# Decoder layer (Mamba, cross-attention, experts) on one core: the first batch's state scans move from the Mamba stage into the attention's opening

## The chip, the cores and the metric

One core of one Trainium2 chip runs the whole layer in one launch. The metric is the device time of a run in microseconds (us), median of the runs shown. Engines are named as the profile names them: PE (TensorE matmul), DVE (VectorE), ACT (ScalarE), POOL (GpSimd), SP (SyncE, which here only issues DMAs).

## The reference, cut to what matters

```
x: (4, 512, 256) f32        ctx: (4, 1601, 256) f32
x = layernorm(x + mamba(x))            # d_inner 512, 16 states, conv 4, dt_rank 16
x = layernorm(x + xattn(ctx, x))       # 16 heads of 64; keys = [LN(ctx); LN(x)], 2113 of them
x = layernorm(x + experts(x))          # 8 experts, top 2, and 2 shared

mamba:  xz = x @ W_in.T ; conv, silu ; dt = softplus(...) ; B, C per state
        for t: h = exp(dt*A) * h + dt*B*xs ;  y = sum over 16 states of h*C
        out = (y + xs*D) * silu(z) @ W_out.T
xattn:  kv = [LN(ctx); LN(x)] @ Wkv ; q = LN(x) @ Wq ; softmax(q k / 8) v @ Wout
```

## The kernel before

Three stages follow one another: `mamba`, `attention`, `experts`. Everything is f32; the products of the attention's projections are made from a high and a low f32r part of each operand.

**Mamba stage.** A loop over the four batches (x[0] to x[3]) computes, with 512 channels as four blocks of 128 partitions and 512 tokens along the free axis, the gate z, B and C, y0 = xs*D, dt and du = dt*xs. For the batches 0 to 2 these are stored to DRAM (`kept_z`, `kept_bc`, `kept_y`, `kept_dtu`). For batch 3 (`LAST`) the recurrence is run on the spot: for each of the 16 states PE spreads the rows of B and C over the partitions (L368, through the constant `sel`), ACT copies B and makes the decays (L243, L247), POOL multiplies du by B (L181, 128x2048), DVE runs one scan over 128x2048 (L326) and multiplies by C out of PSUM (L332), and PE sums into `ps_y` through the identity (L423). Then gate, output product (L433), residual and layernorm (L340 to L358).

**Attention stage.** Batches are taken in the order `BATCHES = [3, 0, 1, 2]`, 16 heads each: 64 groups g (batch, head) of 17 key tiles kt, which the text calls slots. All engines walk one list written at trace time, `MADE = BEFORE + BESIDE[g][kt] + AFTER`; an engine skips the items that do not concern it and takes the others strictly in this order. Items: S/A (statistics of context rows), N (normalise rows, L983), T (turn them on PE into `ring`, scale and split on ACT, L852 and L856, low part on DVE, L1008, which is also where `ring_free` is counted up), Q/K/V (projections, L1144), X (PE scores and DVE row maxima over the keys, L1188 and L1042), M (maxima to a row), O (output projection), P (Mamba's output product), G/J/L (norm after Mamba and the latents' statistics), E/F (norm after attention). In the main loop PE makes per slot the scores (L1246, L1247), the items of the slot, and the product with the values three slots back (L1259).

**The scans of the later batches** are spread over the main loop of the batch before, 64 units of 128x512 (unit u: block u//16, state u%16), one every `U_STEP` = 2.85 slots: D(u) is POOL's product with B (L795) and ACT's decay (L882); H(u), two slots later, is DVE's scan (L992) followed on POOL by the product with C (L802) and the addition to `y` (L806). POOL runs D and H in the order of the list, so D(u+1) stands behind H(u). B and C of a unit come by a DMA that spreads two rows over the partitions (`load_bc`, 512 KB per unit).

**The opening of the attention** (`BEFORE`): statistics, N and T of all rows; POOL splits the weights in 12 steps (L818, L820), three per block of four heads, each block stored to DRAM before the buffer is used again; then Q, all K, X, M and six V of the first head.

Of the kernel before, what the change touches and what calls it, by code (L numbers as in the profile page):

```python
# [15 lines left out]
F32 = mybir.dt.float32  # L16
# [6 lines left out]
P = 128  # L23
# [9 lines left out]
KEPT = {}  # L33


def mamba(nc, x, w_in_t, conv_w, conv_b, w_x_t, w_dt_t, b_dt, a_log, d_skip, w_out_t, x1):
# [7 lines left out]
    LAST = B - 1  # L44
# [5 lines left out]
    with ExitStack() as ctx:  # L50
# [7 lines left out]
        ps_y = ctx.enter_context(nc.psum_tensor("m_y", [P, CT, S], F32))  # L58
# [4 lines left out]
        wout = sb("m_wout", [P, CT, DM])  # L63
# [3 lines left out]
        a_neg = sb("m_a", [P, CT, NS])  # L67
        dsk = sb("m_d", [P, CT])
        ident = sb("m_ident", [P, P])
        diag_d = sb("m_diag", [P, CT, P])  # L70
        sel = sb("m_sel", [P, 2 * NS, P], BF16)
        x_in = sb("m_xin", [P, TT, DM])
        x_res = sb("m_xres", [P, TT, DM])
# [6 lines left out]
        xdr = sb("m_xdr", [P, S])  # L80
        xd3 = sb("m_xd3", [P, 3, S], BF16)
# [4 lines left out]
        dA = sb("m_dA", [P, 2, CT, S])  # L86
        bsb = sb("m_bsb", [P, 2, S])
        dbx = sb("m_dbx", [P, 2, CT, S])
        h = sb("m_h", [P, 2, CT, S])
        y0 = sb("m_y0", [P, CT, S])  # L90
        stats = sb("m_stats", [P, TT, 6])
        mv = sb("m_mv", [P, TT, 2])
        rstd = sb("m_rstd", [P, TT])
        half = sb("m_half", [P, TT])

        w_loaded = sem("m_w_loaded")
        a_loaded = sem("m_a_loaded")
        x_loaded = sem("m_x_loaded")
        xres_loaded = sem("m_xres_loaded")
        x_in_free = sem("m_x_in_free")  # L100
        consts_set = sem("m_consts_set")
        a_set = sem("m_a_set")
# [12 lines left out]
        dA_ready = sem("m_dA_ready")  # L115
        dbx_ready = sem("m_dbx_ready")
        h_scanned = sem("m_h_scanned")
        y_added = sem("m_y_added")
        g_ready = sem("m_g_ready")
        var_ready = sem("m_var_ready")  # L120
        rstd_ready = sem("m_rstd_ready")
# [10 lines left out]
        def _(sp):  # L132
# [5 lines left out]
            sp.dma_start(wout[:], w_out_t.rearrange("(c p) n -> p c n", p=P)).then_inc(w_loaded, 16)  # L138
            sp.dma_start(x_in[:], x[0].rearrange("(t p) d -> p t d", p=P)).then_inc(x_loaded, 16)
            sp.dma_start(x_res[:], x[LAST].rearrange("(t p) d -> p t d", p=P)).then_inc(xres_loaded, 16)  # L140
            for b in range(LAST):
                sp.wait_ge(x_in_free, b + 1)
                sp.dma_start(x_in[:], x[b + 1].rearrange("(t p) d -> p t d", p=P)).then_inc(x_loaded, 16)
# [11 lines left out]
            sp.wait_ge(z_kept, 16 * LAST)  # L155
            sp.wait_ge(bc_kept, 32 * LAST)
            sp.wait_ge(y0_kept, 16 * LAST)
            sp.wait_ge(dt_kept, 16 * LAST)
            sp.wait_ge(du_kept, 16 * LAST)

        @block.gpsimd
        def _(pool):
            nc.gpsimd.memset(wx[:], 0.0)
            nc.gpsimd.memset(wdt[:], 0.0).then_inc(consts_set, 1)
            nc.gpsimd.memset(ident[:], 0.0)
            nc.gpsimd.memset(sel[:], 0.0)
            nc.gpsimd.memset(half[:], -0.5)
            nc.gpsimd.memset(xs_pad[:], 0.0)
            nc.gpsimd.memset(dA[:, :, :, 0:1], 0.0).then_inc(consts_set, 1)
            pool.wait_ge(consts_set, 2)  # L170
            nc.gpsimd.affine_select(out=ident[:], in_=ident[:], compare_op=ALU.not_equal, fill=1.0, base=0,
                                    pattern=[[-1, P]], channel_multiplier=1)

            nc.gpsimd.affine_select(out=sel[:], in_=sel[:], compare_op=ALU.not_equal, fill=1.0, base=-DTR,
                                    pattern=[[-1, 2 * NS], [0, P]], channel_multiplier=1).then_inc(consts_set, 1)

            def times_b(n, i):
                pool.wait_ge(act_read, B * AREAD + n + 1)
                if n >= 2:
                    pool.wait_ge(h_scanned, n - 1)  # L180
                nc.gpsimd.tensor_tensor(dbx[:, i], du[:], bsb[:, i:i + 1, :].to_broadcast([P, CT, S]),  # L181
                                        ALU.mult).then_inc(dbx_ready, 1)

            pool.wait_ge(du_ready, B)
            for n in range(NS):
                times_b(n, n % 2)
            pool.wait_ge(var_ready, 1)
            nc.gpsimd.tensor_tensor(rstd[:], mv[:, :, 1], half[:], ALU.pow).then_inc(rstd_ready, 1)

        @block.scalar  # L190
        def _(act):
            act.dma_start(a_neg[:], a_log).then_inc(a_loaded, 16)
            for dst, src in ((cb, conv_b), (bdt, b_dt), (dsk, d_skip)):
                act.dma_start(dst[:], src).then_inc(w_loaded, 16)
            act.wait_ge(a_loaded, 16)
            nc.scalar.activation(a_neg[:], a_neg[:], ACT.Exp).then_inc(a_set, 1)
            act.wait_ge(w_loaded, 16 * 8)
            act.wait_ge(consts_set, 3)
            act.wait_ge(a_set, 2)
            for b in range(B):  # L200
# [19 lines left out]
                if b < LAST:  # L220
                    if b > 0:
                        act.wait_ge(y0_kept, 16 * b)
                    for c in range(CT):
                        a = nc.scalar.activation(y0[:, c], xs[:, c], ACT.Identity, scale=dsk[:, c:c + 1])
                    a.then_inc(y0_ready, 1)
# [11 lines left out]
            act.wait_ge(dt_ready, B)  # L237

            def decay(n, i):
                act.wait_ge(bank_full, B * RING + 2 * n + 1)  # L240
                if n >= 2:
                    act.wait_ge(dbx_ready, n - 1)
                nc.scalar.activation(bsb[:, i], ring[:, i], ACT.Copy).then_inc(act_read, 1)  # L243
                if n >= 2:
                    act.wait_ge(h_scanned, n - 1)
                for c in range(CT):
                    e = nc.scalar.activation(dA[:, i, c, 1:S], dt[:, c, 1:S], ACT.Exp, scale=a_neg[:, c, n:n + 1])  # L247
                e.then_inc(dA_ready, 1)

            for n in range(NS):  # L250
                decay(n, n % 2)

        @block.vector
        def _(dve):
            dve.wait_ge(a_set, 1)
            nc.vector.tensor_scalar(a_neg[:], a_neg[:], -1.0, None, ALU.mult).then_inc(a_set, 1)
            dve.wait_ge(w_loaded, 16 * 8)
            dve.wait_ge(consts_set, 3)
            for c in range(CT):
                last = nc.vector.tensor_scalar(diag_d[:, c], ident[:], dsk[:, c:c + 1], None, ALU.mult)  # L260
            last.then_inc(consts_set, 1)
# [9 lines left out]
            for b in range(B):  # L271
# [20 lines left out]
                if b < LAST:  # L292
                    dve.wait_ge(xd_ready, b + 1)
                    dve.sem_inc(dve_read, 1)
                else:
                    step(nc.vector.tensor_copy(xd3[:, 0], xd))
                    nc.vector.tensor_tensor(xdr[:], xd, xd3[:, 0], ALU.subtract).then_inc(dve_read, 1)
                    dve.wait_ge(dve_read, read + 1)
                    step(nc.vector.tensor_copy(xd3[:, 1], xdr[:]))
                    nc.vector.tensor_tensor(xd3[:, 2], xdr[:], xd3[:, 1], ALU.subtract).then_inc(xd_ready, 1)  # L300
# [19 lines left out]
            def scan(n, i):  # L320
                dve.wait_ge(dA_ready, n + 1)
                dve.wait_ge(dbx_ready, n + 1)
                if n >= 2:
                    dve.wait_ge(y_added, n - 1)

                nc.vector.tensor_tensor_scan(h[:, i].rearrange("p c s -> p (c s)"),  # L326
                                             dA[:, i].rearrange("p c s -> p (c s)"),
                                             dbx[:, i].rearrange("p c s -> p (c s)"),
                                             0.0, ALU.mult, ALU.add).then_inc(h_scanned, 1)
                dve.wait_ge(h_scanned, n + 1)  # L330
                dve.wait_ge(bank_full, B * RING + 2 * n + 2)
                nc.vector.tensor_tensor(h[:, i], h[:, i], ring[:, 2 + i:3 + i].to_broadcast([P, CT, S]),  # L332
                                        ALU.mult).then_inc(dve_read, 1)

            for n in range(NS):
                scan(n, n % 2)

            dve.wait_ge(y_added, NS)
            for c in range(CT):
                g = nc.vector.tensor_tensor(cv[:, c], ps_y[:, c], zs[:, c], ALU.mult)  # L340
            g.then_inc(g_ready, 1)

            dve.wait_ge(xres_loaded, 16)
            for k in range(2):
                dve.wait_ge(bank_full, B * RING + 2 * NS + k + 1)
                r = nc.vector.tensor_tensor(x_res[:, 2 * k:2 * k + 2], ring[:, k].rearrange("p (t d) -> p t d", d=DM),
                                            x_res[:, 2 * k:2 * k + 2], ALU.add)
            step(r)
            for t in range(TT):
                s = nc.vector.bn_stats(stats[:, t], x_res[:, t])  # L350
            step(s)
            for t in range(TT):
                s = nc.vector.bn_aggr(mv[:, t], stats[:, t])
            step(s)
# [7 lines left out]
        def _(pe):  # L362
# [50 lines left out]
            for n in range(2):  # L413
                state_row(n, n)
                state_row(NS + n, 2 + n)
# [1617 lines left out]
```

## Time and profile before

| | us |
|---|---|
| median of 3 runs (3352.40 to 3355.03) | 3353.45 |
| profiled execution | 3351.15 |
| its span | 3349.4 |
| granted clock of PE, mean | 0.957 |

| stretch of the span | what runs | us |
|---|---|---|
| 0 to 180.5 | Mamba, four batches without recurrence | 180.5 |
| 180.5 to 354.9 | recurrence, output product and norm of batch 3 | 174.4 |
| 354.9 to 461.5 | opening of the attention | 106.6 |
| 461.5 to 2895.5 | 64 groups | 2434.0 |
| 2895.5 to 3349.4 | last rows, experts | 453.9 |

PE is busy 90% of the span, DVE 58%, ACT 40%, POOL 29%. An idle time in brackets behind a row is that of the engine just before the instruction, with what ended it. Time of the profiled execution and span differ by 1.75 us, which lie outside the first and the last instruction.

### The profile page before, as it was taken

Reading aid. Unit: us, or ns where it says so; the run is one execution under the profiler, and the core shown is the slowest. Engines: PE = TensorE matmul, PEld = TensorE weight load, DVE = VectorE, ACT = ScalarE, POOL = GpSimd, SP = SyncE. Lnnn points to the kernel's source line nnn. Section 1 sums busy time; section 2 is a strip of 40 time slices with the busy share of each in tenths; the row PEclk is TensorE's granted clock in tenths of the full one; section 3 lists DMA queues with packets and bytes.
Section 4 is the critical chain, followed back from the end, with each engine's and each line's share of the span. In section 5 each row is a group of like instructions: output and inputs, shape, how many; then the busy total and the mean of one; then the engine's idle time right before and its main releaser. Section 6 shows DMA issues by size and latency. Waiting matters only on the chain. (4 is left out here: it accounts for less than half of the span.)

```text
span 3349.4 us, 34358 instructions
## 1 busy us (share of the span) xinstructions
PE 3011.7 (90%) x11690; PEld 1869.2 (56%) x11694; DVE 1942.5 (58%) x3342; ACT 1350.9 (40%) x2320; POOL 965.4 (29%) x760
## 2 busy tenths in 40 slices
PE   6656289999999999999899999999999999899997
PEld 2222155655655565656565655656565666586666
DVE  4699456666565766665566666555545554352225
ACT  4532135445344545453544445344434344321121
POOL 1044336566200656640036556100000000102213
PEclk8878589999999999999999999999999999899998
DMA  3200343343211434331134344210101110221112
GB/s 112 93 0 0 117 129 124 110 132 111 69 36 51 126 104 133 97 93 33 35 104 124 104 126 124 55 35 14 36 14 35 25 30 20 101 100 50 54 39 70
DMA packets 90914, 248.56 MB, mean 74 GB/s; under 512 B 10661, under 2 KB 44585, under 8 KB 83065
## 3 DMA queue, kind: packets, MB, share of 16 engines
q1 hardware_dynamic: 86760, 237.04, 23.0%
q0 software_dynamic: 3408, 9.31, 1.0%
q8 instruction: 96, 1.57, 0.2%
q14 instruction: 74, 0.60, 0.1%
q10 hardware_dynamic: 576, 0.04, 0.0%
HBM read 183.34 MB, written 28.38 MB: 63 GB/s over the span
## 5 line engine op out<-in xcount | busy, mean ns | idle before, releaser
L904 ACT ACTIVATE a_p<-a_st 128x512 f32<-128x512 f32 (+1 forms) x1088 | 649.2, 597 | 1211.4 <-PE a_st L1247 1202.6
L1259 PE MATMUL a_o<-a_p,a_vals 128*65 128x512 f32 (+1 forms) x2176 | 1116.4, 595 | 0.0
L1042 DVE TENSOR_REDUCE a_maxes<-a_mx 128x1 f32<-128x512 f32 x1024 | 674.0, 683 | 114.7 <-PE a_mx L1188 108.3
L1246 PE MATMUL a_st<-a_qd,a_keven 128*128 128x512 f32 (+1 forms) x544 | 435.0, 800 | 0.0
L1246 PE MATMUL a_st<-a_qd,a_kodd 128*128 128x512 f32 (+1 forms) x544 | 432.3, 795 | 0.0
L1247 PE MATMUL a_st<-a_qm,a_kone 65*128 65x512 f32 (+1 forms) x1088 | 431.0, 396 | 0.0
L802 POOL TENSOR_TENSOR a_shared<-a_shared,a_bc 128x512 f32<-128x512 f32 x192 | 245.5, 1279 | 480.1 <-DVE a_shared L992 480.1
L1259 PEld LDWEIGHTS a_o<-a_p,a_vals 128*65 128x65 f32 (+1 forms) x2176 | 288.5, 137 | 124.5 <-issue 2.7
L1247 PEld LDWEIGHTS a_st<-a_qm,a_kone 65*128 65x128 f32 (+1 forms) x1088 | 203.5, 187 | 264.7 <-issue 264.6
L992 DVE TENSOR_TENSOR_SCAN a_shared<-a_shared 128x512 f32<-128x512 f32 x192 | 234.5, 1221 | 178.5 <-POOL a_shared L795 129.7
L795 POOL TENSOR_TENSOR a_shared<-a_dtu,a_bc 128x512 f32<-128x512 f32 x192 | 245.2, 1277 | 198.9 <-DMA a_bc<-m_kept_bc 198.9
L784 POOL TENSOR_TENSOR a_erstd<-a_emv,a_half 128x4 f32<-128x4 f32 x7 | 7.1, 1014 | 920.2 <-DVE a_emv L1068 920.0
L1144 PE MATMUL a_ring<-a_kvh,a_wt 128*128 128x512 f32 (+1 forms) x768 | 228.6, 380 | 27.2 <-POOL a_wt L820 20.8
L806 POOL TENSOR_TENSOR a_y<-a_y,a_shared 128x512 f32<-128x512 f32 x192 | 245.0, 1276 | 15.3
L1188 PE MATMUL a_mx<-a_kodd,a_qd 128*128 128x512 f32 x512 | 219.3, 453 | 30.4 <-DVE a_maxes L1042 30.0
L1188 PE MATMUL a_mx<-a_keven,a_qd 128*128 128x512 f32 x512 | 214.6, 469 | 32.4 <-DVE a_maxes L1042 28.0
L1035 DVE COPY a_vals<-a_ring 128x512 f32<-128x512 f32 (+2 forms) x160 | 97.8, 611 | 234.4 <-PE a_ring L1144 233.6
L1246 PEld LDWEIGHTS a_st<-a_qd,a_keven 128*128 128x128 f32 (+1 forms) x544 | 101.9, 187 | 159.6 <-issue 104.3
L1246 PEld LDWEIGHTS a_st<-a_qd,a_kodd 128*128 128x128 f32 (+1 forms) x544 | 101.1, 186 | 159.2 <-issue 117.7
L1144 PEld LDWEIGHTS a_ring<-a_kvh,a_wt 128*128 128x128 f32 x768 | 141.7, 191 | 67.3 <-issue 21.2
L1144 PE MATMUL a_ring<-a_wt,a_kvh 128*128 128x256 f32 (+1 forms) x1088 | 174.1, 282 | 0.0
L1144 PEld LDWEIGHTS a_ring<-a_wt,a_kvh 128*128 128x128 f32 (+1 forms) x1088 | 158.5, 187 | 14.5
(256 smaller groups left out, 4204.3 us busy)
## 6 DMA issues: line engine op xcount, KB each, us to landing
a_bc<-m_kept_bc SPq DMA_DIRECT2D x192, 512.0 KB, 3.7
a_wt<-a_w_split SPq DMA_DIRECT2D x15, 1536.0 KB, 9.6
a_kone<-a_keven SPq DMA_DIRECT2D x32, 528.5 KB, 5.1
a_kone<-a_kodd SPq DMA_DIRECT2D x32, 528.5 KB, 5.5
e_wall<-in_w_t_dram SPq DMA_DIRECT2D x27, 512.0 KB, 5.6
a_shared<-in_ctx_dram SPq DMA_DIRECT2D x4, 1536.0 KB
a_w_split<-a_wt SPq DMA_DIRECT2D x4, 1536.0 KB, 6.6
a_dtu<-m_kept_dtu SPq DMA_DIRECT2D x12, 512.0 KB, 5.0
```

Source lines behind the costliest of these rows:

```text
L795: nc.gpsimd.tensor_tensor(dbx[:, n % 2], dtu[:, c % 2, 1], bc[:, n % 2, 0], ALU.mult).then_inc(dbx_ready, 1)
L802: nc.gpsimd.tensor_tensor(seen, state[:, n % 2], bc[:, n % 2, 1], ALU.mult).then_inc(seen_ready, 1)
L806: nc.gpsimd.tensor_tensor(y[:, c], y[:, c], seen, ALU.add).then_inc(y_added, 1)
L904: nc.scalar.activation(p[0:r, s % 4], st[0:r, s % 2], ACT.Exp, scale=SCALE).then_inc(exp_done, 1)
L992: nc.vector.tensor_tensor_scan(state[:, n % 2], decay[:, n % 2], dbx[:, n % 2], 0.0, ALU.mult, ALU.add).then_inc(scanned, 1)
L1035: o = nc.vector.tensor_copy(vals[0:r, t * HG:(t + w) * HG, 0:DH], made)
L1042: nc.vector.reduce_max(maxes[:, c, t:t + 1], mx[:, i % 2], AX_X).then_inc(mx_max, 1)
L1144: mm = nc.tensor.matmul(out, x(k), y(k), start=(j == 0), stop=(j == len(terms) - 1))
L1188: mm = nc.tensor.matmul(mx[:, i % 2], qd[of(g)][:, t * P:(t + 1) * P], kk[:, c * 512:(c + 1) * 512], start=True, stop=True)
L1246: nc.tensor.matmul(st[0:r, s % 2], keys_of(g)[:, kt * P:kt * P + r], qd[of(g)][:], start=True, stop=False)
L1247: nc.tensor.matmul(st[0:r, s % 2], k_one[g % 2][0:DH + 1, kt * P:kt * P + r], qm[of(g)][0:DH + 1, :], start=False, stop=True).then_inc(st_ ...
L1259: nc.tensor.matmul(ps_o[0:DH + 1, g % 2], vals[0:r, kt * HG + j, :], p[0:r, s % 4], start=(kt == 0), stop=(kt == KT - 1)).then_inc(pv_done, 1)
```

## The change

The recurrence of batch 3 and everything that served it leave `mamba`; all four batches now only store. In `attention` the units of batch 3 (called b = 0 here) are run within `BEFORE`: three buffers for the inputs and four for the states (`early`, which lies where q, its low part and `k_one` lie later), sums over states on PE through the identity into the banks `st` and `ps_o`, the product with C on DVE, or on POOL for every second unit from u = 24 on. Between the units stand S, A, the 12 weight splits (items W), N, T and U of the context, V 0 to 5 and K 0 to 2. Then come P, G, J, L, the latents' N, T, U, then Q, K 3 and 4, X, M.

For all batches the order of units becomes state by state (unit u: state u//4, block u%4), so that B and C are loaded 16 times per batch instead of 64. H (scan) stands at slot +3 and its sequel C (POOL: product with C in place, addition to y) at +5 as an item of its own. The low part of turned rows becomes item U, two slots behind T, and `ring_free` is counted up by ACT. PE makes the first item of a slot, then the product with the values, then the others.

```diff
 mamba:
-    LAST = B - 1          # and ps_y, wout, sel, diag_d, x_res, xd3, dA, dbx, h, stats ...
+    for b in range(B): ... all of z, bc, y, dt, du stored for every b
-            def times_b(n, i): ...   def decay(n, i): ...   def scan(n, i): ...
-            pe.wait_ge(consts_set, 4)
+            pe.wait_ge(consts_set, 3)
 beside(g):
-            for kind, later in (("D", 0), ("H", 2)):
+            for kind, later in (("D", 0), ("H", 3), ("C", 5)):
...
             at[1 + (3 * i) // 2].append(("T", b + 1, i))
+            at[3 + (3 * i) // 2].append(("U", b + 1, i))
+def first():
+    early = [("S", 0, t) for t in range(CTX_T)] + [("A", 0, i) for i in range(2)]
+    early += [("W", 0, i) for i in range(3 * NG)]
...          # N, T, U of the context, V 0..5, K 0..2; a W behind every second of S, A, N, T, U
+    for u in range(NU + 3):
+        for kind, later in (("H", 1), ("D", 0), ("C", 2)):
+            if 0 <= u - later < NU:
+                made.append((kind, 0, u - later))
+        while done < len(early) and done * (NU - 4) < (u + 1) * len(early):
+            made.append(early[done])
+            done += 1
+    made += [("P", 0, t) for t in range(TT)] + [("G", 0, 0), ("J", 0, 0), ("L", 0, 0)]
...          # latents' N, T, U
+    made += [("Q", 0, 0)] + [("K", 0, i) for i in range(3, len(KC))]
+    return made + [("X", 0, i) for i in range(NX)] + [("M", 0, 0)]
 attention, helpers:
+        def on_pool(u):
+            return u >= 24 and u % 2 == 0
+        def wait_inputs_free(engine, b, u):      # three input buffers for b = 0, two later
+            r = ring_of(b)
+            if u >= r:
+                engine.wait_ge(scanned, unit(b, u) - r + 1)
+            elif b > 0:
+                engine.wait_ge(turned_low, b * len(PREP))
 sync:
+            load_bc(0, 0); load_batch(0); load_rows(0); load_bc(0, 1)     # shortened
...          # load_batch: y, and dt and du of all four blocks, before the context rows
+            def load_gate(b):
+                wait_multiplied(sp, b, NU - 1)
+                sp.dma_start(gate..., KEPT["z"][BATCHES[b]]).then_inc(gate_loaded, 16)
...          # then w_out; after it x of all four batches into x1
 scalar, turn:
                 act.wait_ge(turned_ready, c + 1)
+                act.sem_inc(ring_free[bank(what)], 1)
 vector, scan:
+                if b == 0 and u >= FS:
+                    dve.wait_ge(summed, u - FS + 1)
...
+                nc.vector.tensor_tensor_scan(state_of(b, u), dA, dB, 0.0, ALU.mult, ALU.add).then_inc(scanned, 1)
+                if b == 0 and not on_pool(u):
+                    dve.wait_ge(scanned, u + 1)
+                    nc.vector.tensor_tensor(state_of(b, u), state_of(b, u), bc[:, i % 2, 1], ALU.mult).then_inc(seen_dve, 1)
+            def gate_first():     # before P(0, 0): y = sums + y, y = y * gate, four blocks each
 tensor:
+            def sum_state(u):
+                wait_multiplied(pe, 0, u)
+                nc.tensor.matmul(sums(c), ident[:], state_first[:, u % FS], start=(n == 0), stop=(n == NS - 1)).then_inc(summed, 1)
...
+                    products = [what for what in BESIDE[g][kt] if what[0] in "QKVXMOPT"]
+                    for what in products[:1]:
                         make(what)
                     if g * KT + kt >= LAG:
                         add_o(g * KT + kt - LAG)
+                    for what in products[1:]:
+                        make(what)
```

## Rows read from the trace of the kernel before

**Rows 1.** Windows by stage: start:end, length, busy us of each engine, clock, DMA share, GB/s
```profile
180.51:354.85 174.34, 104.10 (x238) 45.15 (x241) 155.51 (x52) 48.23 (x79) 73.39 (x17) 0.81 0.00 0
354.85:419.93 65.08, 9.02 (x34) 6.02 (x35) 29.48 (x69) 14.92 (x32) 28.14 (x33) 0.50 0.44 151
461.51:2895.50 2433.99, 2343.62 (x9244) 1446.95 (x9242) 1455.73 (x2636) 1103.47 (x1930) 758.76 (x599) 1.00 0.25 74
```

**Rows 2.** Copies of the heads' outputs (one per group): of groups 17-27, and 49-59
```profile
L913 ACT ACTIVATE a_osb<-a_o x11: 582/583/585, 1128.3 to 1504.1; 65x512 f32<-65x512 f32 x11
...
L913 ACT ACTIVATE a_osb<-a_o x11: 582/583/584, 2375.2 to 2732.6; 65x512 f32<-65x512 f32 x11
```

**Rows 3.** Waits (us, times, longest): PE 1128.3-1504.1; PE 2375.2-2732.6; DVE 1128.3-1504.1; PE 1504.1-1717.5
```profile
PE a_mx L1188 <- DVE a_maxes L1042: 12.4, 17, 2.5
...
PE a_mx L1188 <- DVE a_maxes L1042: 2.6, 10, 0.3
...
DVE a_shared L992 <- POOL a_shared L795: 37.1, 16, 4.0
...
PE a_ring L1137 <- DVE a_shared L983: 7.4, 8, 1.7
```

**Rows 4.** Timeline of one unit in the main loop: start, length, instruction, idle before
```profile
528.02 1.27 POOL L802 TENSOR_TENSOR a_shared<-a_shared,a_bc 128x512 f32<-128x512 f32 x1 [1.39 <-DVE a_shared L992]
...
530.61 1.27 POOL L795 TENSOR_TENSOR a_shared<-a_dtu,a_bc 128x512 f32<-128x512 f32 x1
...
531.97 1.23 DVE L992 TENSOR_TENSOR_SCAN a_shared<-a_shared 128x512 f32<-128x512 f32 x1 [3.48 <-POOL a_shared L795]
...
533.27 1.28 POOL L802 TENSOR_TENSOR a_shared<-a_shared,a_bc 128x512 f32<-128x512 f32 x1 [1.39 <-DVE a_shared L992]
```

**Rows 5.** Timeline where DVE and POOL meet, and where each is alone
```profile
194.00 4.54 POOL L181 TENSOR_TENSOR m_dbx<-m_du,m_bsb 128x2048 f32<-128x2048 f32 x1 [4.43 <-DVE m_h L326]
...
196.10 6.72 DVE L326 TENSOR_TENSOR_SCAN m_h<-m_dA,m_dbx 128x2048 f32<-128x2048 f32 x1
...
327.33 4.42 DVE L326 TENSOR_TENSOR_SCAN m_h<-m_dA,m_dbx 128x2048 f32<-128x2048 f32 x1
...
387.57 0.68 DVE L1008 TENSOR_TENSOR a_kvl<-a_shared,a_kvh 128x512 fp32r<-128x512 f32 x1
387.58 1.79 POOL L820 TENSOR_TENSOR a_wt<-a_osb,a_wt 128x512 fp32r<-128x512 f32 x1
...
404.09 0.61 POOL L818 CAST a_wt<-a_osb 128x512 fp32r<-128x512 f32 x1 [0.72 <-DMA a_osb<-in_wkv_dram]
404.78 1.26 POOL L820 TENSOR_TENSOR a_wt<-a_osb,a_wt 128x512 fp32r<-128x512 f32 x1
```

**Rows 6.** Timeline, first instruction of PE in the Mamba stage
```profile
12.64 0.66 PE L379 MATMUL m_ring<-m_ident,m_xin 128*128 128x128 f32 x2 [12.64 <-DVE m_diag L260]
```

**Rows 7.** DMA from 0 to 400 us: GB/s in 40 slices of 10 us; issues with KB, us to landing
```profile
GB/s 250 82 0 105 111 0 257 113 111 1 262 105 111 0 210 2 0 0 0 0 0 0 0 0 0 2 0 0 0 0 0 0 1 0 2 35 193 111 170 210
...
m_kept_dtu<-m_du SPq DMA_DIRECT2D x3, 1024.0 KB, 5.5
...
m_wout<-in_w_out_t_dram SPq DMA_DIRECT2D x1, 512.0 KB, 6.0
```

**Rows 8.** Timeline, DVE after the last sum of batch 3's recurrence
```profile
337.86 2.48 DVE L340 TENSOR_TENSOR m_cv<-m_y,m_zs 128x512 f32<-128x512 f32 x4 [3.79 <-PE m_y L423]
...
353.20 1.38 DVE L358 TENSOR_SCALAR rows<-m_xres,m_mv,m_rstd 128x256 f32<-128x256 f32 x4 [1.15 <-POOL m_rstd L188]
```

**Rows 9.** Timeline of PE in the attention's opening: first Q, first X, M, first score
```profile
419.96 1.19 PE L1144 MATMUL a_ring<-a_kvh,a_wt 128*128 128x512 f32 x2 [20.78 <-POOL a_wt L820]
...
434.78 0.71 PE L1188 MATMUL a_mx<-a_keven,a_qd 128*128 128x512 f32 x2
...
450.80 1.12 PE L1199 MATMUL a_mx<-a_identr,a_mall 128*128 128x128 f32 x4 [0.74 <-DVE a_mall L1048]
...
461.51 0.39 PE L1246 MATMUL a_st<-a_qd,a_keven 128*128 128x512 f32 x1
```

More of the change, by code:

```diff
@@ L219, in _ @@
                 act.wait_ge(xs_ready, (b + 1) * CT)
[L220 to L225, printed above, removed]
+                if b > 0:
+                    act.wait_ge(y0_kept, 16 * b)
+                for c in range(CT):
+                    a = nc.scalar.activation(y0[:, c], xs[:, c], ACT.Identity, scale=dsk[:, c:c + 1])
+                a.then_inc(y0_ready, 1)
                 for c in range(CT):
@@ L335, in _ @@
[L335 to L347, printed above, removed]
@@ L361, in _ @@
         @block.tensor
         def _(pe):
-            pe.wait_ge(w_loaded, 16 * 8)
-            pe.wait_ge(consts_set, 4)
-            def state_row(s, bank):
-                for part in range(3):
-                    mm = nc.tensor.matmul(ring[:, bank], sel[:, s, :], xd3[:, part], start=(part == 0), stop=(part == 2))
-                mm.then_inc(bank_full, 1)
+            pe.wait_ge(w_loaded, 16 * 7)
+            pe.wait_ge(consts_set, 3)
             for b in range(B):
@@ L656, in unit, with late, by_pool, ring_of @@
         def unit(b, u):
+            return b * NU + u
+        def late(b, u):
             return (b - 1) * NU + u
+        def on_pool(u):
+            return u >= 24 and u % 2 == 0
+        def by_pool(u):
+            return sum(on_pool(i) for i in range(u + 1))
+        def ring_of(b):
+            return FR if b == 0 else 2
+        def dtu_of(b, c, i):
+            if c < 2:
+                return dtu[:, c, i]
+            return p[:, 2 * (c - 2) + i] if b == 0 else dtu_two[:, 2 * (c - 2) + i]
+        def inputs(b, u):
+            i = u % ring_of(b)
+            return (decay_first[:, i], dbx_first[:, i]) if b == 0 else (decay[:, i], dbx[:, i])
+        def state_of(b, u):
+            return state_first[:, u % FS] if b == 0 else state[:, u % 2]
+        def wait_inputs_free(engine, b, u):
[4 more added lines that the diff above has]
+                engine.wait_ge(turned_low, b * len(PREP))
+        def wait_multiplied(engine, b, u):
+            if b > 0:
+                engine.wait_ge(seen_ready, late(b, u) + 1)
+            else:
+                if by_pool(u):
+                    engine.wait_ge(seen_pool, by_pool(u))
+                engine.wait_ge(seen_dve, u + 1 - by_pool(u))
         @block.sync
@@ L821, in _ @@
                                         ALU.subtract).then_inc(raw_split, 1)
-                if i == 2:
-                    make_rstd(("A", 0, 1))
-                    make_rstd(("L", 0, 0))
+            for what in BEFORE:
+                if what[0] == "D":
+                    times_b(*what[1:])
+                elif what[0] == "C":
+                    times_c(*what[1:])
+                elif what[0] == "W":
+                    split(what[2])
+                elif what in POW:
+                    make_rstd(what)
             for g in range(NH):
```

421 lines of the change are left out of this document (180 added, 241 removed).

## The prediction

> **What bounds the kernel now.** I read the windows by stage first. In the 64 groups PE is busy 2343.6 of 2434.0 us at full clock [rows 1]: PE bounds this stage, and only its waits can be won. The recurrence and tail of batch 3 (174.3 us) and the opening before the first Q (65.1 us) are different: DVE is busy 155.5 of 174.3 us in the one, and in the other no engine reaches half [rows 1]. The reader is to see two stretches run one after the other in which different things are scarce. This is what the change lays on top of each other.
>
> Then the main loop's waits. Ten groups that carry units of the next batch last 1504.1 - 1128.3 = 375.8 us, the same ten of the last batch, without units, 2732.6 - 2375.2 = 357.4 us [rows 2]. Of these 18.4 us, 12.4 - 2.6 = 9.8 us are PE waiting for row maxima [rows 3], and those come late because DVE, in order, waits 37.1 us in the same stretch for POOL's product with B before a scan [rows 3]. The timeline of a unit shows why: product with C at 528.02, addition, product with B at 530.61, scan at 531.97, next product with C at 533.27 [rows 4]. It is a ring of four instructions of 5.25 us, and a unit is due every 2.85 slots: a group of 17 slots takes 357.4/10 = 35.7 us, so a slot 2.1 and a unit 6.0 us on average, less in the quick groups. The ring has no room left there. A second wait of PE, 7.4 us in the groups after them, is for normalised rows before they are turned [rows 3].
>
> Last, what DVE and POOL do to each other. A scan of 128x2048 takes 4.42 us alone and 6.72 us when it starts at 196.10 under a POOL product that runs to 198.54; it ends 4.28 us after that product [rows 5]. The other way round, a weight split that takes 1.26 us alone takes 1.79 us when a DVE subtraction (0.68 us, two SBUF operands) starts 0.01 us earlier, and ends 1.12 us after it [rows 5]. Both times the late one does its whole work after the first, less 0.14 us. These two engines work side by side only in name when both read two SBUF operands.
>
> **The change, part by part.**
>
> Mamba stage, start. PE begins at 12.64 us, released by the diagonals, which waited for the constant `sel` [rows 6]. Both go. Next in the way is x, behind the weights: the output weights, issued at 2.96 us, landed 6.0 us later [rows 7], and x takes their place in the queue, so PE starts near 9.1: -3.5 us. Bounds 0 and -7.
>
> Recurrence out. du of batch 3 is ready at 180.5 [rows 1], now at 177. Storing it takes 5.5 us [rows 7] and the stage waits for it: the attention starts at 182.8. Five small loads (2.4 us of issues, an estimate), then B and C, y, dt and du, 3.5 MB, at the 250 GB/s of the busiest slices [rows 7] 14 us and 2 for latency: the first product with B at 201. The first statistics item stands before the first scan on DVE and needs the context rows, 1.6 MB more, 6.6 us: first scan at 208. Before, it ran at 185, so 23 us of loading stand open now.
>
> The 64 units with the work beside them. Alone, DVE's sum is 64 scans x 1.23 + 44 products x 0.68 = 108.6 us and some 27 for statistics, norms, low parts, V and K: 136. POOL's is 84 products x 1.27 + 12 splits x (0.61 + 1.26) = 129 and two roots, 132. If they ran side by side the phase would last about 140. By the rows of meetings they take turns, each instruction costing its length less 0.14: scans 64 x 1.09 = 69.8; POOL's products 84 x 1.13 = 94.9; DVE's products 44 x 0.54 = 23.8; splits 12 x (0.47 + 1.12) = 19.1; low parts 7 x 0.54 = 3.8; norms and root 5 (estimate). Sum 216 us [rows 4, 5]. What does not read two operands (statistics, V and K out of PSUM) hides beside POOL. Three products with B are made before the first scan: -3. Stalls: by the same turns the old recurrence should take 4.28 + 4.54 - 0.14 = 8.7 us a state, and DVE's busy time there, 155.5 us [rows 1] less some 7 of tail, is 9.3; and for V and K DVE waits in order until PE (and ACT) have made them, nine times 1 to 3 us. I take 19, between 0 and 35. The last product with C ends at 208 + 216 - 3 + 19 = 440 us.
>
> Here the Trainium skill speaks against the change. Its page "SBUF — State Buffer", section "Who interferes with whom", says that a DVE instruction with two SBUF inputs contends with a GpSimd instruction that reads SBUF. The trace agrees, by the two meetings above. The section "SBUF: two separate sides" of that page says that the loser fully blocks for the whole instruction; the rows show 0.14 us less than that.
>
> After the units. From the gate product to the norm's end the old tail took 353.20 + 1.38 - 337.86 = 16.7 us [rows 8]. New in it: the gate is loaded only after the last unit (+5), four additions of the sums (+2.4), and x of four batches queues behind gate and weights (+3, bounds 0 and 6). Latents' statistics, norms, turns: 12 us (estimate from the same work interleaved before). From Q to the first score it took 461.51 - 419.96 = 41.6; six V after M (451.9 to 461.5: -9.6) and three of five K (-6, of 14.8 up to the first X) are already made: 26 [rows 9]. Together 27 + 12 + 26 = 65. The first score comes at 505 instead of 461.5 [rows 9]: **+43 us**. Bounds: no stalls and the low ends, +18; stalls 35 and late x, +62.
>
> So the overlap gains nothing here: 174 us of recurrence and tail and 65 of opening were 239 and become about 280, since the old kernel's products with C read PSUM and ran freely beside POOL, while the new ones take turns, and most of the opening's own work was short.
>
> Main loop, units. With H at +3 and C at +5, POOL makes D(u+1) before C(u); the ring is cut. POOL's load stays 3 x 1.27 = 3.8 us per unit of 5.4 to 7.7, and its next product is ready about 3.7 slots before the scan wants it. DVE's scan can now meet a POOL product (up to 1.13 us), which two `a_mx` banks absorb. Excess of 18.4 us per batch [rows 2] shrinks to about 3: **-15 x 3 = -45**. Bounds: -10 and -55 in all.
>
> Low parts later: DVE no longer waits for ACT between two N, and PE's 7.4 us per batch [rows 3] shrink to 2: **-5 x 3 = -15**, bounds 0 and -22. PE's order within a slot: the products are the same, 0 (0 to -3; PE stays the bound, so a wait must vanish for a gain). 48 loads of B and C fewer per batch: 0, DMA is busy a quarter of the stage [rows 1]. If that cover were absent it could only help. The opening loads of batch 1 (3.5 MB at slot 0) are issued behind Q, some 27 us before the first score, and hide.
>
> Sum on the profiled execution: +43 - 45 - 15 = -17 us, 3351.15 to 3334. The median stands 2.3 us above this execution: 3336.5.
>
> **The rivals.**
>
> A, the late one of two always waits for the other's whole length: then the phase is 64 x 1.23 + 84 x 1.27 + 44 x 0.68 + 12 x 1.87 + 7 x 0.68 + 5 = 248 instead of 216, +32: 3368, slower. It decides where each turn's start is not overlapped, that is where an engine waits on a semaphore and not on the other's instruction. For it: each DVE product waits for its own scan. Against it: the 0.14 us in both rows [rows 5]. The page of the Trainium skill named above, "SBUF — State Buffer", states this form of the rule.
>
> B, DVE and POOL run side by side after all (short instructions interleave): phase 140 to 150 instead of 232, -85: 3250. For it: no row shows two 128x512 products meeting often. Against it: both rows.
>
> C, the loop does not give back what the ring seems to cost, since scans that never met POOL now meet two products each and the row maxima stay late; this gain is 10 instead of 60: 3386, slower. For it: DVE is busy 1456 of 2434 us and POOL's share does not fall [rows 1]. Against it: the 37.1 us of DVE waits are all for the ring [rows 3].
>
> **How the numbers follow.** No change is told from one of 0.2%, 6.7 us, either way: 3346.7 to 3360.1. Forecast 0.67, of which 0.53 faster, 0.08 same, 0.06 slower, its own range 3310 to 3362. A 0.14 (0.01 faster, 0.03 same, 0.10 slower), B 0.07 (faster), C 0.12 (slower). Sums: faster 0.61, same 0.11, slower 0.28. Range: low end +18 for the opening with -57 for the loop, 3314, and a step towards B: 3298. High end: A and the stalls with the loop as forecast, 3374; B and most of C stay out.
>
> **What the changed profile would show.** First scan near 208; the units until 440, with scans whose mean lies near 1.6 to 1.9 us instead of 1.23 and POOL products near 1.7 instead of 1.27. If their means stay at 1.23 and 1.27, the turns are wrong and B is right. First score near 505. In the ten groups with units, length near 361 instead of 375.8 and no DVE wait for POOL's product with B; if the length stays, C. PE's wait for normalised rows under 3 us a batch. The prediction fails by the opening if the stalls exceed 35 us, and by the loop if the ring was not the cause.

## The result and the profile after

The changed kernel takes 3302.07 us (3295.86 to 3304.08, 4 runs) against 3354.24 for the kernel before, ratio 0.984, 95% interval 0.982 to 0.986: 52 us or 1.6% faster. The forecast was 3336.5, 17 us faster, so the sign was right and the size a third of what came. The profiled executions stand 47.9 us apart (spans 3349.4 and 3301.5), and the account below is made between them.

Windows by stage of the changed kernel (start:end, length, busy us of each engine with counts, granted clock, DMA share, GB/s): Mamba, loading, the units, from the last unit to the first score, the 64 groups, the rest.

```profile
0.00:179.62 179.62, 109.28 (x224) 46.68 (x224) 95.91 (x104) 87.14 (x109) 3.36 (x9) 0.82 0.29 105
179.62:204.23 24.61, 0.00 (x0) 0.00 (x0) 2.44 (x6) 3.80 (x6) 4.50 (x10) 0.50 0.86 305
204.23:435.02 230.79, 125.91 (x241) 48.41 (x242) 200.63 (x167) 56.22 (x88) 166.87 (x106) 0.65 0.23 74
435.02:499.60 64.58, 34.25 (x87) 21.17 (x86) 32.65 (x68) 8.45 (x18) 2.02 (x2) 0.58 0.39 129
499.60:2847.60 2348.00, 2324.75 (x9242) 1448.89 (x9242) 1528.80 (x2635) 1101.75 (x1931) 813.88 (x600) 1.00 0.16 44
2847.60:3301.50 453.90, 406.44 (x1798) 297.35 (x1798) 179.98 (x438) 89.04 (x156) 93.36 (x97) 0.93 0.24 76
```

The first score comes at 499.6 instead of 461.5 [rows 9]: the move alone loses 38.1 us. From there to the last head's copy the loop takes 2348.0 instead of 2434.0 us [rows 1]: it gains 86.0. The last stage is 453.9 in both. 38.1 - 86.0 = -47.9.

The copies of the heads' outputs, for the same ten groups with units and the same ten without as in [rows 2]:

```profile
L869 ACT ACTIVATE a_osb<-a_o x11: 582/582/586, 1136.1 to 1496.3; 65x512 f32<-65x512 f32 x11
...
L869 ACT ACTIVATE a_osb<-a_o x11: 582/582/583, 2328.7 to 2684.9; 65x512 f32<-65x512 f32 x11
```

360.2 against 375.8 us with units, 356.2 against 357.4 without. The same copies give the whole loop by regions:

| per batch, us | before | after | difference |
|---|---|---|---|
| ten groups with units, batches 1 to 3 of the loop | 376.6, 375.9, 376.1 | 360.3, 360.2, 360.2 | -48 |
| four groups with norm, context rows, turns | 167.6 each | 157.0, 157.0, 157.1 | -32 |
| two groups to the next batch | 81.0, 81.1, 78.7 | 79.0 each | -4 |
| last batch, 14 groups | 498.4 | 497.0 | -1 |

The waits of PE (us, times, longest) after, first over the ten groups, then over the six that follow; they answer to [rows 3]:

```profile
PE a_mx L1171 <- DVE a_maxes L1018: 2.8, 6, 0.8
...
PE a_mx L1171 <- DVE a_maxes L1018: 1.3, 3, 0.8
PE a_ring L1117 <- DVE a_shared L939: 0.6, 1, 0.6
```

Waits of DVE over the ten groups after: for the product with B, 37.1 us before [rows 3], there is left

```profile
DVE a_shared L952 <- POOL a_shared L739: 3.5, 3, 1.2
```

The units' phase is the stretch from the first scan (204.23) to the end of the last product with C (435.02). Groups of instructions in it (count, busy us, mean ns, idle before with releasers): scans, products with C on DVE, products with B on POOL, and with C on POOL.

```profile
L952 DVE TENSOR_TENSOR_SCAN a_early<-a_early 128x512 f32<-128x512 f32 x64 | 109.7, 1724 | 18.8 <-POOL a_early L739 8.7 <-issue 6.9 <-ACT a_early L838 2.9
L956 DVE TENSOR_TENSOR a_early<-a_early,a_bc 128x512 f32<-128x512 f32 x44 | 58.3, 1326 | 4.6
...
L739 POOL TENSOR_TENSOR a_early<-a_p,a_bc 128x512 f32<-128x512 f32 x31 | 52.0, 1680 | 3.5 <-DVE a_early L952 3.5
...
L747 POOL TENSOR_TENSOR a_early<-a_early,a_bc 128x512 f32<-128x512 f32 x20 | 34.2, 1710 | 24.4 <-DVE a_early L952 24.4
L767 POOL CAST a_wt<-a_osb 128x512 fp32r<-128x512 f32 x12 | 11.8, 980 | 26.5 <-DMA a_w_split<-a_wt 21.8 <-DMA a_osb<-in_wq_dram 4.7
```

A scan of 1.23 us lasts 1.72 on average here, a DVE product of 0.68 us 1.33, a POOL product of 1.27 us 1.6 to 1.7. These are not longer instructions, they are instructions that wait for the other engine. Of the 38 scans that start under a POOL instruction 37 end 1.08 to 1.09 us after it, of 35 DVE products 34 end 0.54 to 0.55 us after it. Of the instructions with one SBUF tensor the statistics (L905) do not wait, the 8 that start under a POOL instruction end before it; the normalising of rows (L939) does, 12 of 13 end 0.15 us after POOL's, with a mean of 1.21 us against 0.50 in a_dve_all, where POOL only splits weights.

### The profile page after: what moved, and what is told of

Same layout as the page of the kernel before. It is cut to its first block and busy times, and to the rows that moved or that the text cites. A ratio compares the mean times of both kernels' runs of the same rounds, so it can differ in the third digit from the quotient of the medians.

```text
span 3301.5 us, 33908 instructions
## 1 busy us (share of the span) xinstructions
PE 3000.6 (91%) x11590; PEld 1862.5 (56%) x11590; DVE 2040.4 (62%) x3415; ACT 1346.4 (41%) x2307; POOL 1084.0 (33%) x824
## 5 line engine op out<-in xcount | busy, mean ns | idle before, releaser
L1241 PE MATMUL a_st<-a_q,a_kone 65*128 65x512 f32 (+1 forms) x1088 | 430.6, 396 | 0.0
L1240 PE MATMUL a_st<-a_q,a_keven 128*128 128x512 f32 (+1 forms) x544 | 326.0, 599 | 0.7 <-issue 0.7
L1240 PE MATMUL a_st<-a_q,a_kodd 128*128 128x512 f32 (+1 forms) x544 | 314.7, 578 | 0.0
L1171 PE MATMUL a_mx<-a_kodd,a_q 128*128 128x512 f32 x512 | 298.3, 599 | 7.3 <-DVE a_maxes L1018 6.2
L952 DVE TENSOR_TENSOR_SCAN a_shared<-a_shared 128x512 f32<-128x512 f32 x192 | 287.7, 1500 | 13.1 <-POOL a_shared L739 12.0
L1171 PE MATMUL a_mx<-a_keven,a_q 128*128 128x512 f32 x512 | 277.0, 588 | 12.9 <-DVE a_maxes L1018 10.2
L1241 PEld LDWEIGHTS a_st<-a_q,a_kone 65*128 65x128 f32 (+1 forms) x1088 | 202.1, 186 | 152.8 <-issue 128.7
L739 POOL TENSOR_TENSOR a_shared<-a_dtu,a_bc 128x512 f32<-128x512 f32 x96 | 146.6, 1528 | 169.2 <-DMA a_bc<-m_kept_bc 169.2
L1171 PEld LDWEIGHTS a_mx<-a_keven,a_q 128*128 128x128 f32 x512 | 97.9, 191 | 162.9 <-DVE a_maxes L1018 64.6
L1240 PEld LDWEIGHTS a_st<-a_q,a_keven 128*128 128x128 f32 (+1 forms) x544 | 101.4, 186 | 132.5 <-issue 94.2
```

The source lines that it names most:

```text
L739: nc.gpsimd.tensor_tensor(inputs(b, u)[1], dtu_of(b, c, 1), bc[:, i % 2, 0], ALU.mult).then_inc(dbx_ready, 1)
L952: nc.vector.tensor_tensor_scan(state_of(b, u), dA, dB, 0.0, ALU.mult, ALU.add).then_inc(scanned, 1)
L1171: mm = nc.tensor.matmul(mx[:, i % 2], qd[of(g)][:, t * P:(t + 1) * P], kk[:, c * 512:(c + 1) * 512], start=True, stop=True)
L1240: nc.tensor.matmul(st[0:r, s % 2], keys_of(g)[:, kt * P:kt * P + r], qd[of(g)], start=True, stop=False)
L1241: nc.tensor.matmul(st[0:r, s % 2], k_one[g % 2][0:DH + 1, kt * P:kt * P + r], qm[of(g)][0:DH + 1, :], start=False, stop=True).then_inc(st_ ...
```

## The experiments

Kernels whose name begins with b_ start from the kernel before, those with a_ from the changed one. Each was timed beside runs of the kernel before, and the ratio is to those. "Ten" and "four" are the regions of the table above, of the middle batch. Four kernels have the same code up to the first group (changed kernel, a_ring, a_low_at_turn, a_order); their phases differ by 4 us, so less than that is not to be read from this column.

| kernel | us | ratio to before, 95% | ten | four | units' phase |
|---|---|---|---|---|---|
| b_chain_cut | 3407.48 | 1.0155 (1.0138-1.0172) | 397.1 | 167.6 | |
| b_cut_bc4 | 3296.24 | 0.9838 (0.9818-0.9858) | 361.3 | 167.5 | |
| b_bc4 | 3326.31 | 0.9927 (0.9911-0.9944) | 369.3 | 167.6 | |
| b_low_later | 3330.14 | 0.9917 (0.9899-0.9936) | 380.9 | 158.0 | |
| b_order | 3346.06 | 0.9968 (0.9958-0.9978) | 376.7 | 168.5 | |
| b_loop | 3263.35 | 0.9732 (0.9713-0.9751) | 360.5 | 157.2 | |
| changed kernel | 3302.07 | 0.9841 (0.9824-0.9858) | 360.2 | 157.0 | 230.8 |
| a_ring | 3328.22 | 0.9927 (0.9911-0.9944) | 366.6 | 157.0 | 226.6 |
| a_low_at_turn | 3327.36 | 0.9919 (0.9899-0.9939) | 360.9 | 166.5 | 229.4 |
| a_order | 3312.05 | 0.9872 (0.9852-0.9892) | 361.6 | 158.0 | 230.2 |
| a_dve_c | 3303.36 | 0.9843 (0.9826-0.9859) | 360.9 | 157.1 | 232.4 |
| a_dve_all | 3276.18 | 0.9770 (0.9753-0.9786) | 360.9 | 157.0 | 207.3 |
| a_c_psum | 3267.55 | 0.9745 (0.9729-0.9762) | 360.9 | 157.0 | 193.7 |
| a_c_psum_store | 3254.36 | 0.9707 (0.9686-0.9728) | 360.1 | 157.1 | 182.7 |

**The ring of a unit.** In each expectation "theory 1" is the account under test and "rival 2" the other one. First the cut alone, in the kernel before:

```diff
-            for kind, later in (("D", 0), ("H", 2)):
+            for kind, later in (("D", 0), ("H", 3), ("C", 5)):
-                        elif what[0] == "H":      # POOL: product with C and addition
+                        elif what[0] == "C":
```

> The kernel before, with only H at +3 and its sequel C as an item of its own at +5. Theory 1 (the ring of product with B, scan, product with C, addition made the row maxima late): the ten groups with units fall from 376 to 360 to 362 us in each of three batches, the four groups after them stay at 167.6, time 3353 - 47 = 3306. Rival 2 (the scans now meet POOL's products, and it was the order on PE or the shorter load of B and C that helped): the ten groups stay above 370 and the time above 3335.

It became 21 us a batch slower (18 in the third). That lies within the bounds of rival 2 (ten groups above 370, time above 3335), but neither theory had named a slowdown, and the waits of POOL point at another cause. They follow for the kernel before (1128 to 1504) and for this one over its ten groups (1144.4 to 1541.6):

```profile
POOL a_shared L795 <- DMA a_bc<-m_kept_bc: 6.0, 3, 3.0
...
POOL a_shared L795 <- DMA a_bc<-m_kept_bc: 118.4, 53, 6.3
```

POOL waits 53 times for B and C. A unit's buffer becomes free with its product with C; the load is issued then and takes 3.6 us to land (3.7 in the kernel before), and the unit after next cannot begin before. With C three slots later this second ring, buffer, load, product with B, became the longer one. So I gave the loads room:

```diff
-        bc = sb("a_bc", [P, 2, 2, S])
+        bc = sb("a_bc", [P, 4, 2, S])
-                if n >= 2:
-                    sp.wait_ge(seen_ready, n - 1)
+                if n >= 4:
+                    sp.wait_ge(seen_ready, n - 3)
-                            if slot == max(0, int((u - 1) * U_STEP)):
+                            if slot == max(0, int((u - 3) * U_STEP)):
```

> The kernel before with H at +3 and C at +5, as b_chain_cut, and with four buffers for B and C instead of two, so that a load starts two units earlier. Theory 1 (cut alone, the ring only moved: product with C frees the buffer, the load lands 3.7 us later, and then POOL can make the next product with B): POOL no longer waits 116 us per ten groups for loads, the ten groups fall from 397 to 360 to 364 us and the time to about 3306. Rival 2 (it is the meetings of scans with POOL's products that cost 20 us a batch in b_chain_cut): the ten groups stay near 395 and the time near 3400.

361.3 us a batch and 3296.24 in all, and POOL's waits over its ten groups are for scans alone, which is slack:

```profile
POOL a_shared L802 <- DVE a_shared L992: 107.8, 41, 5.7
```

Theory 1 holds, rival 2 falls: the scans still meet POOL's products, and the 20 us are gone. The other side, the changed kernel with `("H", 2), ("C", 2)`:

> The changed kernel with H and C both at +2 as before, units still state by state. Theory 1 (the ring of product with B, scan, product with C, addition makes the row maxima late): ten groups back from 360 to 374 to 378 us in each batch, time 3302 + 45 = 3347. Rival 2 (four times fewer loads of B and C give the gain, the ring's order costs nothing): ten groups stay at 360 to 364, time below 3315.

366.6: between the two. Theory 1 is wrong in size, rival 2 too: only 6.4 of 15.7 us come back with the ring. The remainder had to lie in the order state by state. What that order could give, more room for the loads, was tried in the kernel before, with four buffers and H and C both at +2:

> The kernel before with four buffers for B and C instead of two and loads two units earlier; H and C at +2 as before, so the ring stays. Theory 1 (with two buffers a load that lands late also stops the ring, which cannot catch up; the state-by-state order cured this as a side effect): ten groups from 376 to 366 to 368, as in a_ring, time 3353 - 27 = 3326. Rival 2 (state by state helped in another way, or the order of H and C is all of it): ten groups stay at 374 to 377, time above 3345.

369.3: nearer to theory 1 (366 to 368) than to rival 2, and 7 us of the 9 to be explained. So the account of the 16 us a batch is: 7 for loads with more room (in the changed kernel a side effect of loading once per state), 8 for the cut (369.3 to 361.3), and the cut needs the first. DVE's wait for the product with B, on which the prediction built, is 37.3 us in b_bc4 as it was before, and 4.7 in b_cut_bc4: it goes with the cut alone. The ten groups of a_ring are 2.7 us shorter than those of b_bc4; PE's order, worth 1.4 there (a_order below), may be part of that, the rest stays unassigned.

The two groups to the next batch follow the ring as well: 81.0, 81.1 and 78.7 us in b_bc4, as before, and 78.7 each in b_cut_bc4.

**The low parts.** Alone in the kernel before:

```diff
             at[1 + (3 * i) // 2].append(("T", b + 1, i))
+            at[3 + (3 * i) // 2].append(("U", b + 1, i))
-                dve.sem_inc(ring_free[bank(what)], 1)      # in low_rows, DVE
+                act.sem_inc(ring_free[bank(what)], 1)      # in turn, ACT, after its last read
```

> The kernel before, with only the low parts of turned rows two slots later and the banks released by ACT. Theory 1 (the step was mis-sized: DVE waiting for ACT delays the row maxima and the next norm, more than PE's 7.4 us of waits for normalised rows show): the four groups that carry norm and turns fall from 167.6 to 157 to 159 in each batch, -27 to -32 us in all, 3322 to 3326. Rival 2 (only the recorded waits go, and the rest came from PE's order): 162 a batch, -15 to -18 in all, 3336.

158.0, 158.0 and 159.7 in the three batches: theory 1 by the groups, while the time of 3330 stands 4 us above its range. The medians are 26 us apart. The profile is of the slowest of the four executions (3334.47): in it the four groups are 27 us shorter in sum, but the ten (376.5, 380.9, 378.7) are 7.5 and the two 2.9 us longer, and no run says why. PE's waits over the six groups were 7.4 us for normalised rows [rows 3] and 3.8 for row maxima before (1504.1 to 1717.5); with the lag alone (1498.9 to 1702.5) the first is gone and the second hardly changed:

```profile
PE a_mx L1188 <- DVE a_maxes L1042: 3.8, 6, 1.7
...
PE a_mx L1189 <- DVE a_maxes L1043: 3.0, 6, 1.7
```

The undoing in the changed kernel put U into T's slot and left the release with ACT:

> The changed kernel with the low part on DVE back in the slot of the turn (banks still released by ACT). Theory 1 (the lag of two slots gives the gain, since DVE waits for ACT in order and the next norm and the row maxima stand behind): four groups from 157 to 163 to 167, +18 to +30 in all. Rival 2 (ACT releasing the bank early gives it, PE no longer waits for DVE to free a bank): four groups stay at 157 to 159, +0 to +6 in all.

165.8, 166.5, 165.8: +27 us in the four groups, +25 in the time, theory 1 again, so the lag gives the gain and not the release. DVE's waits for ACT's high part, in order of kernel: before (1504.1 to 1717.5), changed (1496.3 to 1699.1), a_low_at_turn (1502.8 to 1705.5).

```profile
DVE a_kvl L1008 <- ACT a_kvh L856: 16.9, 10, 2.6
...
DVE a_kvl L984 <- ACT a_kvh L813: 1.4, 1, 1.4
...
DVE a_kvl L984 <- ACT a_kvh L813: 16.3, 10, 2.7
```

**PE's order in a slot.** `products[:1]`, product with the values, `products[1:]`, alone in the kernel before, then undone in the changed one:

> The kernel before, with only the order on PE: first item of the slot, product with the values, the other items. Theory 1 (order alone frees nothing, since PE is the bound and DVE still sits in its waits): 0 to -5 us, 3348 to 3354. Rival 2 (the order gives the waits for row maxima time): ten groups -3 to -8 a batch and four groups -4 to -6 a batch, -20 to -40 in all.

> The changed kernel with PE's old order in a slot (all items, then the product with the values). Theory 1 (the order is worth little once scans and low parts are out of the way, as alone in the kernel before, where the groups did not move): 0 to +6 us in all. Rival 2 (it gave the part of the gain in the four groups that the recorded waits did not show): four groups 157 to 160 or more, ten groups +2 or more, +12 to +25 in all.

Alone it moved the groups by less than 2 us either way. The time fell by 10 us (0.3%), twice what theory 1 allowed and half of rival 2's least; the copies of the heads do not account for it, the last one comes 2.7 us earlier and the stretch behind it is 3.1 us shorter in the profiled execution. Undone, the ten groups lose 1.4 us a batch, the four 1.1, 1.0 and 2.6, the two nothing clear and the last batch 1.4, 10.4 us from the first to the last copy: more than theory 1 expected, less than rival 2. So the order is worth some 10 us of time either way; where they lie is shown only for the changed kernel.

**The loop without the move.** b_cut_bc4, b_low_later and b_order together. Units stay block by block here; the four buffers stand in for the order state by state:

> The kernel before with the three edits of the main loop and without the move: H at +3 and C at +5 with four buffers for B and C, low parts later with ACT releasing the banks, PE's order. Theory 1 (the change is a loss of 38 us in the opening and a gain of 85 in the loop): groups as in the changed kernel (ten groups 360, four groups 157, two groups 79), first score where it was (461), time 3302 - 37 = 3265. Rival 2 (part of the loop's gain needs the move, for instance by less DMA traffic): ten groups or the four groups stay 3 us or more above the changed kernel's, time 3275 or more.

Theory 1: the groups are those of the changed kernel to 0.4 us, the first score stands at 459.6. The recurrence's move is a loss of 41 us by the spans (3301.5 and 3260.1), 39 by the medians, and the edits around it are the whole gain.

**Turns between DVE and POOL.** All products with C on DVE (`on_pool` returns False):

> The changed kernel, with all 64 products with C of the first batch on DVE (before: 20 of them on POOL). Theory 1 (DVE and POOL take turns, each instruction costing its length less 0.14 us whoever makes it): 20 x (1.13 - 0.54) = 12 us less from first scan to the end of the last product with C, 231 to 219, and the time 3302 to 3290. Rival 2 (they work side by side, and DVE with 136 us is the fuller one): 20 x 0.68 = 14 us more, 245, time 3315.

232.4 us, neither. The turns are there (scan 1.44, product 1.44 us in the mean; 50 products end 0.54 to 0.55 us after a POOL instruction), but the sum of turns, with the three products made before the first scan taken off, is 213 us in the changed kernel and 202 here, and the phase exceeds it by 17 us there and by 31 here. POOL now waits 70 us for scans and DVE is busy 207 of 232. The likely reading, argued and not tried: the sum holds only while POOL has work waiting that can run beside DVE's copies and statistics; with too little on POOL these stand in the open. Next, the operand C in PSUM, with all products with C on DVE as in a_dve_c, from which it differs in nothing but this:

```diff
+                if b == 0 and c == 0:              # ACT, in decays
+                    nc.scalar.activation(mx[:, n % 2], bc[:, n % 2, 1], ACT.Copy).then_inc(c_ready, 1)
-                    nc.vector.tensor_tensor(state_of(b, u), state_of(b, u), bc[:, i % 2, 1], ALU.mult)
+                    nc.vector.tensor_tensor(state_of(b, u), state_of(b, u), mx[:, n % 2], ALU.mult)
```

> The changed kernel, all 64 products with C of the first batch on DVE, and their operand C copied by ACT once per state into the free PSUM banks a_mx, so that they read one SBUF operand. Theory 1 (the turns are taken only by instructions with two SBUF operands on DVE): DVE's products fall from 1.3 to 1.4 us to 0.69, the phase from first scan to last product with C from 231 to about 190 us (turns 70 + 72 + 19 + 9 = 170, and 20 of stalls), time 3302 - 40 = 3262. Rival 2 (any DVE instruction is held up by POOL, or DVE's order and its waits for V and K set the length): the phase stays above 220, time above 3290.

```profile
L958 DVE TENSOR_TENSOR_SCAN a_early<-a_early 128x512 f32<-128x512 f32 x64 | 97.8, 1528 | 16.8 <-POOL a_early L740 9.1 <-issue 7.4
...
L962 DVE TENSOR_TENSOR a_early<-a_early,a_mx 128x512 f32<-128x512 f32 x64 | 44.0, 688 | 7.0 <-DVE a_early L958 0.5
```

The products last 0.69 us, no longer than with POOL idle, while the scans, still with two SBUF operands, go on taking turns at 1.53. Phase 193.7, 39 us less than a_dve_c and 37 less than the changed kernel, 35 us of time: theory 1. Then both products on DVE:

> The changed kernel with the first batch's products with B and with C all on DVE, so that POOL only splits weights there. Theory 1 (turns): DVE alone has 64 x (1.23 + 0.64 + 0.64) + 27 = 188 us, the splits' turns add up to 19 and stalls some 10: 205 to 217 instead of 231, time 3302 - 20 = 3282. Rival 2 (side by side): DVE's 188 us and the 17 us of waits that it had add to at least 205 as well, but its instructions, and not POOL's, are now the bound, and moving work to it cannot bring more than the 17 us of waits; the means of scan and product would not fall from 1.72 and 1.33 us, where theory 1 has 1.25 and 0.70.

```profile
L948 DVE TENSOR_TENSOR_SCAN a_early<-a_early 128x512 f32<-128x512 f32 x64 | 81.5, 1274 | 2.6
...
L952 DVE TENSOR_TENSOR a_early<-a_early,a_bc 128x512 f32<-128x512 f32 x64 | 48.1, 752 | 7.0 <-DVE a_early L948 0.5
L961 DVE TENSOR_TENSOR a_early<-a_dtu,a_bc 128x512 f32<-128x512 f32 x31 | 23.8, 767 | 0.0
```

207.3 us, theory 1: one engine doing it all is 23 us quicker than two that take turns. Last, on top of a_c_psum, each block of split weights is stored right behind its third split and not one item of the list later, since POOL waits for these stores (21.8 us in the changed kernel, the row of L767 above):

> a_c_psum with each block of split weights stored right behind its third split instead of one item of the list later (POOL waited 4.0, 8.9 and 7.6 us for the stores, DVE then for POOL). Theory 1 (these waits stand in the open, since DVE has at most three units of products with B ahead): phase from 194 to 180 to 187 us, time 3267 - 10 = 3257. Rival 2 (they are covered by DVE's backlog): phase 190 or more, time within 4 us of a_c_psum.

182.7 us, theory 1. It is the best version: 3254.36 us, 2.9% under the kernel before, and 9 us under b_loop (3263.35) timed on the same chip. a_c_psum by itself (3267.55) still stands 4 us above b_loop, so the move of the recurrence pays only with both: DVE's products with C no longer taking turns with POOL, and the stores earlier.

## Why the prediction was right and wrong

**Mamba stage.** PE starts at 8.7 us, forecast 9.1, and the last product of the stage ends at 179.6, forecast 177. ACT's table load of 1.28 us, which the old kernel did at 2.7 us for an exponential that is gone, now stands after the first turn at 9.9 us, and 1.3 us of the start is lost by it. Between kernels with the same Mamba stage this end varies from 176.4 to 179.6, so no more than that is to be read from it.

**Loading.** First scan at 204.2, forecast 208. The rate was taken too low: the window before it shows 305 GB/s in the mean, its idle start included, where 250 was taken.

**The units.** Forecast 216 - 3 + 19 = 232 us, measured 230.8. The price of a turn out of two meetings of instructions, its length less 0.14 us, is right for scans and DVE products, and rival B (side by side, 140 to 150) is out. Rival A, whole lengths, has 248 - 3 = 245 us before any stall, and is out too. That the total came within 1 us is in part luck: the 19 us of stalls were an estimate between 0 and 35. The Trainium skill, "SBUF — State Buffer", section "Who interferes with whom", has the rule by operands: two SBUF inputs on DVE contend with a GpSimd instruction that reads SBUF, at most one does not, outside the modes that use two ports. This trace agrees on the first half (scans and products), and a_c_psum on the second for the product with C (0.69 us). One SBUF operand alone does not make an instruction safe, as the 1.21 us of the normalising show. a_dve_c shows that the sum is not a law: moving work by it missed by 13 us (219 forecast, 232.4 measured).

**From the last unit to the first score.** Forecast 65, measured 64.6, of which 25.0 from the first Q on (forecast 26). The first score: forecast +43, measured +38.1. The prediction's "about 280" for recurrence and opening together does not follow from its own terms: from 177 to the first Q at 479 they give 302, and 295 was measured (179.6 to 474.6).

**The loop's units.** Forecast 376 to 361 a batch and -45 in all; measured 360.2 and -48. The number was right, in part by luck, and its reason incomplete. The prediction cut the ring by H and C and costed the loads at 0 ("48 loads of B and C fewer per batch: 0"), because DMA was busy a quarter of the stage; this step failed in its mechanism, and the total hid it. By the runs, the cut without room for the loads costs 21 us a batch, and the state-by-state order, priced at nothing, is what gave them room (in 1128 to 1504 of the changed kernel POOL has no wait for B and C). What bounded the load was not DMA's share but the 3.6 us from issue to landing, standing in a ring. Nor did the 5.25 us of [rows 4] show a full ring, since the closest units stand 5.4 us apart by the prediction; what shows that it cost 8 us is b_bc4 against b_cut_bc4. Rival C (scans meeting POOL's products keep the row maxima late) is out: b_chain_cut came to such a time by another cause.

**Low parts later: the step that failed in size.** The prediction had DVE's wait for ACT as the mechanism, which the runs bear out, and let PE's 7.4 us per batch shrink to 2, -15 us in all with bounds 0 and -22. Measured, the four groups give 10.6 a batch, 32 in all, outside the bounds. By the runs with one edit each the lag is worth 8 to 10 a batch (27 in all), PE's order, priced at 0 to -3, another 1 to 2.6 here. What the sum missed in the lag can be read from b_low_later, 9.6 us in the middle batch: the residue of 2 was a guess, and nothing of the 7.4 is left; 0.8 of the 3.8 us of waits for row maxima, which stand in the same answer, went too; and some 1.4 us were in no recorded wait of PE. In the changed kernel all these waits together fell from 11.2 to 2.3 us. The two groups to the next batch (4, by the cut of the ring) and the last batch (1, by PE's order), costed at nothing, complete the sum: 48 + 32 + 4 + 1, with 1 before the first copy.

In all, against the forecast: opening 5 us better, units 3, four groups 17, the rest 6; 17 + 31 = 48. The high end of the range, 3374, does not follow from its terms either: rival A alone is 3368, and with stalls of 35 us instead of 19 it is 3384.

## What to carry to other kernels

Where VectorE and GpSimd run long chains with two SBUF operands each, start from the sum of their times (213 us here) and not from the larger (136): the phase took 231. Look for an operand that can lie in PSUM before looking for a better split between the engines. When a ring of instructions is cut, list every buffer that its instructions free and the landing time of what refills it: an edit that lengthens a buffer's life can make a transfer the new ring, here with DMA busy 35% of the time (b_chain_cut). A change with several edits should be priced edit by edit; here the edit in the title was a loss, and the small ones around it were the gain.

## What the runs showed of the hardware that was not expected

An instruction that waits for the other engine ends its own length less 0.14 us after it, for a scan of 2048 elements [rows 5] as for the scans of 512 (1.08 to 1.09 us after) and the DVE products (0.54 to 0.55) of the phase. The 48 products of POOL that start there under a scan, a product or a low part of DVE end 1.05 to 1.16 us after it, of 1.27 alone. In the phase of units PE's granted clock is 0.65 of full speed and its sums of 128x512 last 0.97 us; it did not matter there, since PE was busy 126 of 231 us. The phase with both products on DVE alone still has means of 1.27 and 0.75 us, near their lengths alone, with 12 weight splits beside it.
